# Transposing the row maxima by DMA instead of TensorE and a ScalarE copy

## The reference

```python
x = x + attn_a(_layernorm(x), Wq, bq, Wk, bk, Wv, bv, Wo)      # 16 heads, entries (0, last) and (last, 0) masked
x = x + ffn(_layernorm(x), gate_w, down_w, down_b, up_w, up_b) # top 2 of 8 experts by the mean over tokens, gelu
x = x + attn_b(_layernorm(x), w_qkv, w_out)
x = x + ffn(_layernorm(x), gate_w, down_w, down_b, up_w, up_b)

scores = einsum('bhqd,bhkd->bhqk', q, k) * scale
weights = jax.nn.softmax(scores, axis=-1)
out = einsum('bhqk,bhkd->bhqd', weights, v)
```

## Time and profile before

| | us |
|---|---|
| median of 3 runs | 932.47 (931.51 to 935.10) |
| profiled execution | 931.88 |
| its span, first to last instruction | 930.1 |
| TensorE busy in the span | 861.5 |
| VectorE busy | 781.5 |
| ScalarE busy | 757.5 |
| GpSimd busy | 539.8 |
| DMA queue of SyncE, share of 16 engines | 24.8% |

### The profile page before, as it was taken

The page is one execution under the profiler, slowest core; times in us unless marked ns, Lnnn a source line. Parts: engine busy times, 40 slices in busy tenths (PEclk is TensorE's granted clock), DMA queues, the critical chain, the costliest instruction groups (busy, mean ns, idle before and its releaser), DMA issues.

```text
span 930.1 us, 32135 instructions
## 1 busy us (share of the span) xinstructions
PE 861.5 (93%) x12592; PEld 444.0 (48%) x12592; DVE 781.5 (84%) x1410; ACT 757.5 (81%) x1305; POOL 539.8 (58%) x1086
## 2 busy tenths in 40 slices
PE   3699999999999999999999999999999999998875
PEld 1244444444445454455545445455554554554434
DVE  2889999999998989989898998989889888889533
ACT  2278888888888888888988898888898888897864
POOL 7345555545664766647565674657576485653432
PEclk9989999999999999999999999999999999999987
DMA  3354233222222222212222221222223133132001
GB/s 107 119 159 142 79 89 102 83 74 67 78 78 76 60 80 68 83 50 80 78 72 70 66 83 58 83 66 82 59 71 99 47 102 95 54 104 64 4 24 46
DMA packets 89862, 72.16 MB, mean 78 GB/s; under 512 B 5040, under 2 KB 72784, under 8 KB 89680
## 3 DMA queue, kind: packets, MB, share of 16 engines
q1 hardware_dynamic: 89280, 69.52, 24.8%
q10 hardware_dynamic: 432, 0.59, 0.2%
HBM read 39.68 MB, written 29.88 MB: 75 GB/s over the span
## 4 chain that ended last, share of the span: by engine, by line
PE 66%; DVE 18%; issue 8%; ACT 4%; POOL 2%; DMA 1%; POOLq 0%; SPq 0%; DVEq 0%; ACTq 0%
PE values_bank L829 19%; DVE nmax L643 14%; PE ring L840 11%; PE ring L850 10%; PE m_bank L816 9%; PE m_bank L977 4%; PE m_bank L1010 3%; PE ring L880 3%; PE ring L903 3%; ACT probs L717 2%; PE m_bank L950 1%; PE ring L895 1%; DMA wb<-in_attn_b 0%; DVE x L631 0%; DVE x L678 0%
## 5 line engine op out<-in xcount | busy, mean ns | idle before, releaser
L643 DVE TENSOR_REDUCE nmax<-ring 128x4 f32<-128x1024 f32 x512 | 603.7, 1216 | 46.6 <-PE ring L840 44.5
L717 ACT ACTIVATE probs<-ring 128x1024 f32<-128x1024 f32 x512 | 520.7, 1034 | 35.6 <-PE ring L850 32.9
L829 PE MATMUL values_bank<-probs,values 128*32 128x256 f32 x4096 | 277.0, 384 | 1.7 <-ACT probs L717 1.7
L850 PE MATMUL ring<-q_stack,k_stack 32*128 32x256 f16 x2048 | 198.4, 273 | 14.1 <-DVE nmax L643 14.0
L537 POOL TENSOR_SCALAR xy<-x,mv,rstd 128x128 f32<-128x128 f32 x256 | 201.7, 798 | 7.9
L840 PE MATMUL ring<-k_stack,q_stack 32*128 32x256 f16 x2048 | 183.2, 277 | 15.3 <-DMA k_stack<-scratch 5.1
L515 POOL TENSOR_SCALAR mparts<-nmax 128x32 f16<-128x32 f32 x64 | 14.1, 220 | 279.1 <-DVE nmax L643 279.0
L829 PEld LDWEIGHTS values_bank<-probs,values 128*32 128x32 f32 x4096 | 123.9, 109 | 63.8 <-issue 23.8
L850 PEld LDWEIGHTS ring<-q_stack,k_stack 32*128 32x128 f16 x2048 | 64.4, 92 | 132.7 <-issue 73.7
L840 PEld LDWEIGHTS ring<-k_stack,q_stack 32*128 32x128 f16 x2048 | 52.9, 93 | 115.4 <-ACT probs L717 41.2
L781 ACT COPY values<-m_bank 128x128 f32<-128x128 f32 x128 | 28.9, 278 | 60.3 <-PE m_bank L816 59.0
(11 more groups left out here) (118 smaller groups left out, 959.7 us busy)
## 6 DMA issues: line engine op xcount, KB each, us to landing
scratch<-parts SPq DMA_DIRECT2D x384, 64.0 KB
q_stack<-scratch SPq DMA_DIRECT2D x64, 256.0 KB, 2.6
k_stack<-scratch SPq DMA_DIRECT2D x64, 256.0 KB, 3.0
out<-x SPq DMA_DIRECT2D x16, 256.0 KB, 3.0
x<-in_x SPq DMA_DIRECT2D x3, 768.0 KB, 6.5
q_stack<-maxT SPq DMA_DIRECT2D x128, 8.0 KB
x<-in_x SPq DMA_DIRECT2D x1, 896.0 KB, 6.7
x<-in_x SPq DMA_DIRECT2D x1, 640.0 KB, 5.3
```

Source lines behind the costliest of these rows:

```text
L643: nc.vector.tensor_reduce(dst, src, axis=AX.X, op=ALU.max, negate=True).then_inc(max_done, 1)
L717: nc.scalar.activation(probs[g % 2][:, c:c + 2, :, :], pair_of("exps", n, p)[:, :, :].rearrange("p x (k q) -> p x k q", k=TILES), ACT.Exp) ...
L829: last = nc.tensor.matmul(values_bank[32 * c:32 * (c + 1), a * TOKENS:(a + 1) * TOKENS], values[turn % RING][:, k, PER_GROUP * g + c, :], ...
L850: last = nc.tensor.matmul(pair_of("exps", turn, p)[:, a, k * TOKENS:(k + 1) * TOKENS], k_stack[r][rows, of // 2, k * P:(k + 1) * P], q_sta ...
```

## The change

The parts of the maxima, 32 columns, are padded with zeros to 128 columns. SyncE transposes them with two DMA transposes per turn (128 by 128 fp16 each) from `mparts` to `maxT`, both in SBUF; the two TensorE transposes, the ScalarE copy and the fp16 identity go away. SyncE now waits for GpSimd's `mparts_ready` in place of `maxT_ready`, then for the landing of its own two transposes (`maxT_in`), before it issues the two transfers to q_stack. ScalarE's wait for `max_in` of the turn two before moves to SyncE.

```diff
-        mparts = [sb(f"mparts{i}", [P, TILES, MAX_PARTS * HEADS], FP16) for i in range(2)]
-        maxT = [sb(f"maxT{i}", [MAX_PARTS * HEADS, TOKENS], FP16) for i in range(2)]
+        mparts = [sb(f"mparts{i}", [P, TILES, P], FP16) for i in range(2)]
+        maxT = [sb(f"maxT{i}", [P, TOKENS], FP16) for i in range(2)]
...
-            nc.scalar.copy(identh[:, :], ident[:, :])
...
+            for m in mparts:
+                nc.gpsimd.memset(m[:, :, MAX_PARTS * HEADS:], 0.0)
...
-                        sp.wait_ge(maxT_ready, (n + 1) + 1)
+                        sp.wait_ge(mparts_ready, (n + 1) + 1)
+                        if live(n - 1):
+                            sp.wait_ge(max_in[(n - 1) % 2], (n - 1) // 2 * 32 + 32)
+                        for t in range(TILES):
+                            sp.dma_start(maxT[(n + 1) % 2][:, t * P:(t + 1) * P], mparts[(n + 1) % 2][:, t, :], transpose=True).then_inc(maxT_in[(n + 1) % 2], 16)
+                        sp.wait_ge(maxT_in[(n + 1) % 2], (n + 1) // 2 * 32 + 32)
...
-                            pool.wait_ge(mT_done, (n - 1) + 1)
+                            pool.wait_ge(maxT_in[(n - 1) % 2], (n - 1) // 2 * 32 + 32)
...
-                    if p == 0 and live(n + 1):
-                        act.wait_ge(mT_done, (n + 1) + 1)
-                        if live(n - 1):
-                            act.wait_ge(max_in[(n - 1) % 2], (n - 1) // 2 * 32 + 32)
-                        nc.scalar.copy(maxT[(n + 1) % 2][:, :],
-                                       m_bank[:, :].bitcast(FP16)[0:MAX_PARTS * HEADS, 0:TOKENS]).then_inc(maxT_ready, 1)
...
-                    if p == 1 and live(n + 1):
-                        if batch_at(n, 2) is None and batch_at(n, 3) is None:
-                            fill_m(pe, maxT_ready, (n + 1) + 1)
-                        pe.wait_ge(mparts_ready, (n + 1) + 1)
-                        for t in range(TILES):
-                            last = nc.tensor.transpose(m_bank[:, :].bitcast(FP16)[0:MAX_PARTS * HEADS, t * P:(t + 1) * P],
-                                                       mparts[(n + 1) % 2][:, t, :], identh[:, :])
-                        last.then_inc(mT_done, 1)
```

More of the change, by code:

```diff
@@ L101, in build @@
         ident = sb("ident", [P, P])
-        identh = sb("identh", [P, P], FP16)
         ones = sb("ones", [P, P])
@@ L322, in build @@
         mhi_done, mrest_done, mparts_ready = sem("mhi_done"), sem("mrest_done"), sem("mparts_ready")
-        mT_done, maxT_ready = sem("mT_done"), sem("maxT_ready")
+        maxT_in = [sem(f"maxT_in{i}") for i in range(2)]
         max_in = [sem(f"max_in{i}") for i in range(2)]
```

## The result

| | before | changed |
|---|---|---|
| median, us | 933.26 (931.51 to 935.10, 4 runs) | 940.55 (938.17 to 941.94, 4 runs) |
| profiled execution, us | 931.88 | 941.01 |
| its span, us | 930.1 | 939.2 |

The changed kernel takes 1.0075 of the time of before, 95% interval 1.0045 to 1.0105. It is slower, by 7 us (4 to 10 by the interval), which is under one per cent. Forecast was 943, 11 us slower.

A forecast was written before the change was run, and what follows sets the result against it. TensorE with VectorE's reductions was taken to bound the kernel, SyncE's queue having slack. Profiled 931.9, less 3 for TensorE's gain, plus 14 for SyncE's lengthened loop, gave 943 us; the 8 in 10 range was 927 to 985.

The forecast's parts named there:

- The bound: Whole kernel: TensorE with VectorE's reductions sets the end; SyncE's queue is off the path, with 211.7 us of waits.
- TensorE's gain, value -3: TensorE's removed transposes: 1 us from 50 plain steps plus 2 us from steps with routing work; bounds 0 to 15 us.
- rival 2: TensorE and VectorE do not tie, so TensorE's whole share returns: -15 us at best, 917 to 927; chance 0.08.
- ScalarE's copy, value 0: ScalarE's 64 removed copies, 22.2 us, are covered by TensorE's L829, so removing them gives nothing.
- X, value 4.3: SyncE's time from issuing the first transpose until both have landed: 4.3 us, between 3.2 and 7.2.
- The price, value +14: SyncE's lengthened loop: 12 us over turns 1 to 19, 1.8 us once for turn 0, nothing later.
- the prediction's formula: SyncE's price in turns 1 to 19: 18 x (8.71 + X - 12.34), the loop against the mean step.
- The 8.71: SyncE's loop per step without the transposes, in us: loads 0.84, two transfers 1.16, six writes 3.40, then 3.31 to next loads.
- The slack of the later steps: SyncE's loop of 13.01 us fits the mean step of 13.66 between turns 19 and 63, so nothing is lost there.
- The two pages: Skill pages on DMA transposes: one gave an X of 4.8 and some 23 us, the other 3.5 and no cost.
- The signs named in advance: Changed profile: X 4 to 5 us, q_stack waits of some 0.7 us in turns 1 to 19, none later.
- rival 1: SyncE's X stays under about 3.7, all hidden and only the gain left: 930 us, 927 to 934; chance 0.30.

The follow-up runs named there:

- gain_only: Changed kernel without the two DMA transposes and the wait for them, maxT zero throughout; 926.75 us, 0.9922 of the kernel before.
- no_copy: Kernel before with only ScalarE's copy of maxT left out, maxT zero; 934.86 us, ratio 1.0003.
- plain_copies: Changed kernel with the two transposes of a turn replaced by two ordinary copies into tiles nobody reads; 930.43 us, 0.9963 of the kernel before.
- cost_only: Kernel before, TensorE's transposes and ScalarE's copy kept, with the two DMA transposes and SyncE's wait added into unread tiles; 945.66 us, ratio 1.0127.
- first_20: Changed kernel with the transposes issued ahead of the q_stack and k_stack loads in turns 0 to 19 only; 926.23 us, 0.9921 of the kernel before.
- four_transposes: Changed kernel with each of the two transposes issued twice and SyncE waiting for all four; 1076.07 us, 1.1511 of the kernel before.
- transposes_first: Changed kernel with the two transposes issued ahead of the q_stack and k_stack loads in every turn; 925.83 us, 0.9919 of the kernel before.

## Why the prediction came out right, step by step

**The bound.** That the end was TensorE's with VectorE's, and SyncE's queue beside it with slack, held: the wait of 211.7 us on it was the slack, and it is what the change spent.

**TensorE's gain, value -3.** Right in kind, mis-sized. The trace of gain_only is 5.45 us ahead at turn 63, and the ratio says 7.3 (4.6 to 9.9). The term had 0.02 us in each of 50 plain steps, 1 us, since VectorE's bound was to take the rest. Nineteen steps of the first attention gave 0.10 each, by way of ScalarE's `qk`, which the working did not see; the plain steps of the second gave nothing. For the steps with routing work it had 2 us. The steps that differ from plain ones gave up to 0.37 each, and two near the end 0.53 and 0.59, together some 4. This term is most of why the kernel is 7 us slower and not the forecast's 11. That the whole 15 us of rival 2 would not come held.

**ScalarE's copy, value 0.** Shown by no_copy, within 2 us.

**X, value 4.3.** Measured 3.54 in the median and 3.96 in the mean, 4.0 or more in 23 of 64 turns, at most 5.29. The value was too high, the range from 3.2 to 7.2 held it. For two plain copies the working had 3.5, and 3.2 as the lower bound; plain_copies shows 2.79 in the median.

**The price, value +14.** The lateness is 13.11 us at turn 19, which has that stretch's gain in it already, and 14.00 in cost_only, which has none. The sum was right by luck: two of its terms were off by 0.4 us a step each, in opposite directions. From load to load the changed kernel took 13.00 us on average in turns 2 to 21 ((285.48 - 38.47) / 19), where the prediction had 13.01. But X is 3.90 of it, not 4.3, and the rest is 9.10, not 8.71. With the X of these steps, the prediction's formula would have given 18 x (8.71 + 3.90 - 12.34) + 1.5 = 6; the other 7 are 18 x 0.39. The 8.71 was read from one step at 440 us. Its four pieces, there and on average in these 19 steps: up to the maxima 0.84 and 1.09, the two transfers 1.16 and 1.29, the six writes 3.40 and 3.48, from their end to the next loads 3.31 and 3.24. So two things were missing: some loads of k_stack take 1.3 to 1.6 us to issue in place of 0.43 (turns 7, 17 and 19), and 0.1 us passes between two issues. The constants and items of x that SyncE also loads in the first steps (2.37 us for gate_w, 2.20 for down_w) lie mostly inside the wait for the writes' landing: that piece is 3.74 in turns 2 to 5 and 3.11 in the fifteen that follow.

**The slack of the later steps.** "For the 44 later steps nothing" held, and first_20 shows it. The formula came near at a larger X too: at 6.7 it gives 18 x 3.07 + 44 x 1.75 + 4.2 = 136, and four_transposes, with 6.7, costs 145. There the loop is the step itself, and the sum is the number of turns times the loop's excess over 13.07. A free X was thought to reach up to 3.6; by the measured rest and the plain step it ends at 12.24 - 9.10 = 3.1, which is an estimate, and plain_copies, with a mean X of 3.18 and still 3.9 us of price, agrees.

**The two pages.** "VectorE: DVE Perf Modes" of the Trainium skill, section "The three transpose paths", led to an X of 4.8; measured was 3.54, so its 1.3 us do not come on top of what copies take (2.79); it is 0.75 more. "Advanced Engine Details and Errata" of the Trainium skill, section "X-Bar Transpose (TRN2)", has transposing DMAs as fast as regular ones: for the transfer itself the traces come near to that (2.7 us from issue to landing against 2.5 for plain_copies), for the issue they don't (1.22 against 0.59), and the issue is what stood in the loop.

**The signs named in advance.** One was missed: X was to be 4 to 5 us, and its median is 3.54. That is even below the 3.7 under which rival 1 had everything hidden, and still the kernel is slower; the fault is the 8.71 again. L436 stands right behind L425, as named. The first exponential sides of turns 1 to 19 were to wait for q_stack<-maxT for some 0.7 us each, and none after: 13 of these 19 wait, 0.86 us on average, and turn 0 waits 1.86; none after turn 19 does. The transposes stand in the chain up to 289 us and not later, as named. Plain steps after turn 20 were to be shorter by at most 0.1 us: they are, by 0.10 in the first attention and 0 in the second.

## What to carry to other kernels

A queue that issues transfers in order and waits for their landing is an engine with a loop of its own: add up issue, landing and what the landing releases, and hold the sum against the shortest steps that follow each other, not against the mean. Read the loop from several steps, with the gaps between the issues, and where it is fullest: one step at 440 us gave 8.71 for what took 9.10 on average in turns 2 to 21. When a wait for a landing must go into such a queue, put the issue where the queue idles anyway (behind the last step's writes, while they land), and the wait as late as its user allows: here the same transfers then cost nothing (0.9919 of the time before, against 0.9922 without them).

## What the runs showed of the hardware

A DMA transpose of 128 by 128 fp16 within SBUF holds SyncE for 1217 ns in the median, against 590 for a copy of the same tile, and lands 2.7 us after its issue:

```profile
L421 SPq DMA_TRANSPOSE maxT<-mparts x128: 1094/1217/2678, 39.3 to 881.1; - x128
...
DMA to landing us min/median/max: 2.2/2.7/5.1
```

The landing has a tail, up to 5.1 us, which makes X 4 to 5.3 in a third of the turns. The copies had it too (X up to 4.92), so it is not the transposition's. What is in the way then was not found. The loads of 256 KB issued just ahead don't explain it: in transposes_first, where they come behind, the two transposes took as long to land (4.08 in the mean).
